# Graph attention on TensorE: exponentials as weights in column tiles of 32, V with a column of ones as 65 streaming columns

## What is computed

```
h  = max(layernorm(x), 0)                            # x is 4096 x 64
scores = (h W a1)[:, None] + (V W a2)[None, :]       # V = entity_embs, 4096 x 64
e  = where(scores > 0, scores, 0.2 scores); where(adj > 0, e, -9e15)
x  = x + elu(softmax(e, axis=1) @ V + h)
h2 = max(layernorm(x), 0)
x  = x + relu((adj.T @ h2) @ U.T / adj.sum(axis=0)[:, None])
```

## Time and profile before

| | |
|---|---|
| median of 3 runs | 402.12 us (400.76 to 402.92) |
| span of the profiled execution, first to last instruction | 399.7 us |
| the runs' times and that span | the span is 2.4 us below the median, 1.1 below the fastest run |
| PE busy | 350.8 us, 88% |
| DVE busy | 305.2 us, 76% |
| ACT busy | 258.7 us, 65% |
| POOL busy | 154.5 us, 39% |
| mean granted TensorE clock | 0.973 of 2.4 GHz |
| PE instructions | 7003 matmuls, 7003 weight loads |

### The profile page before, as it was taken

One profiled execution on the slowest core, in us unless ns is written; L12 is line 12 of the kernel. 1 busy time (PEld: TensorE's weight loads), 2 busy tenths in 40 slices (PEclk: granted clock), 3 DMA queues, 4 the chain that ended last, 5 costly groups with the idle time before them and its releaser, 6 DMA issues.

```text
span 399.7 us, 15175 instructions
## 1 busy us (share of the span) xinstructions
PE 350.8 (88%) x7003; PEld 220.2 (55%) x7003; DVE 305.2 (76%) x419; ACT 258.7 (65%) x322; POOL 154.5 (39%) x136
## 2 busy tenths in 40 slices
PE   1716999799999888889999989989997899999996
PEld 0712565454445464535455534445544448999996
DVE  8799899759998598889967989998889761307433
ACT  2402699799997888799889999967775760110000
POOL 8775385584220771130051130032569682210000
PEclk9958699999999999999999999999999999999999
DMA  9999999999999999971000010002001004201110
GB/s 168 130 108 109 108 107 114 130 107 108 109 139 104 105 107 104 103 83 50 2 4 3 4 55 3 3 8 53 3 3 29 2 4 80 55 2 32 41 23 18
DMA packets 26806, 25.18 MB, mean 63 GB/s; under 512 B 22041, under 2 KB 22105, under 8 KB 26742
## 3 DMA queue, kind: packets, MB, share of 16 engines
q0 software_dynamic: 4752, 16.90, 40.7%
q1 hardware_dynamic: 19830, 6.75, 7.7%
q10 hardware_dynamic: 2160, 0.56, 0.8%
HBM read 72.76 MB, written 2.11 MB: 187 GB/s over the span
## 4 chain that ended last, share of the span: by engine, by line
PE 44%; DVE 25%; POOL 10%; issue 9%; ACT 6%; DMA 5%; SPq 0%; POOLq 0%; DVEq 0%
DVE scratch L882 15%; PE w L1249 13%; PE q L1364 10%; PE q L1224 9%; PE den L1257 4%; PE w L1364 4%; DMA adj_sb<-in_adj_dram 3%; POOL adj_sb L425 3%; DVE arena L934 3%; ACT q L724 2%; ACT arena L710 2%; DMA bi<-rows_sb 1%; PE den L1364 1%; POOL adj_sb L429 1%; POOL stat_c L470 1%
## 5 line engine op out<-in xcount | busy, mean ns | idle before, releaser
L882 DVE CUSTOM_DVE_ANT_0 scratch<-adj_sb,t_row 125x2048 uint8<-125x2048 uint8 x66 | 152.9, 2317 | 4.6 <-DMA adj_sb<-in_adj_dram 1.7
L1249 PE MATMUL w<-arena,v_sb 128*32 128x500 f32 (+3 forms) x1120 | 128.8, 508 | 2.3 <-issue 1.3
L1224 PE MATMUL q<-bi,adj_sb 128*32 128x125 bf16 (+1 forms) x3360 | 93.1, 220 | 15.2 <-ACT q L724 7.7
L1224 PEld LDWEIGHTS q<-bi,adj_sb 128*32 128x32 fp8e4 (+1 forms) x3360 | 70.8, 97 | 63.6 <-ACT q L724 32.2
L706 ACT ACTIVATE arena<-q,t_col 128x1000 f32<-128x1000 f32 (+2 forms) x102 | 88.4, 871 | 7.9 <-PE q L1224 7.6
L1257 PE MATMUL den<-arena,ones 128*32 128x250 f32 (+1 forms) x960 | 80.5, 342 | 0.0
L1257 PEld LDWEIGHTS den<-arena,ones 128*32 128x32 f32 x960 | 38.2, 111 | 49.8 <-issue 45.2
L710 ACT ACTIVATE arena<-arena,t 128x1000 f32<-128x1000 f32 (+2 forms) x38 | 40.8, 1073 | 18.6 <-DVE arena L934 18.4
L724 ACT ACTIVATE q<-second_row,minus_b 128x750 f32<-128x750 f32 (+1 forms) x49 | 48.1, 981 | 1.3
L724 ACT ACTIVATE q<-arena,minus_b 128x375 f32<-128x375 f32 (+1 forms) x53 | 42.3, 800 | 1.3
L1364 PE MATMUL q<-g_all,adj_sb 124*128 124x129 f16 (+1 forms) x660 | 39.2, 220 | 0.0
(11 more groups left out here) (186 smaller groups left out, 376.8 us busy)
## 6 DMA issues: line engine op xcount, KB each, us to landing
adj_sb<-in_adj_dram POOLq DMA_DIRECT2D x33, 500.0 KB, 37.0
arena<-s_dram SPq DMA_DIRECT2D x2, 500.0 KB, 7.8
out_dram<-v_sb SPq DMA_DIRECT2D x10, 96.0 KB, 1.9
x_sb<-in_x_dram SPq DMA_DIRECT2D x1, 928.0 KB
v_sb<-x_dram SPq DMA_DIRECT2D x1, 768.0 KB, 5.3
v_sb<-n_L_gnn_entity_embs_dram ACTq DMA_DIRECT2D x2, 256.0 KB, 5.7
v_sb<-n_L_gnn_entity_embs_dram SPq DMA_DIRECT2D x2, 256.0 KB, 4.8
second_row<-s_dram SPq DMA_DIRECT2D x1, 500.0 KB, 4.3
```

The lines of the kernel that those rows point to most:

```text
L882: nc.vector.tensor_tensor_reduce(out=junk[0:R, :], in0=adj_bytes[0:R, b, half], in1=t_row[0:R, half], scale=1.0 / ONE, scalar=0.0, op0=ALU ...
L1224: last = nc.tensor.matmul(q[n % Q_SLOTS][e:e + width, bank, start:start + R], weights, bi[:, i % BI_SLOTS, k, :], start=not ON_ACT[n] and ...
L1249: last = nc.tensor.matmul(att(i)[h * D + d:h * D + d + 32, 0:(k1 - k0) * R], v_sb[:, c, d:d + 32], e[:, k0 * R:k1 * R], start=first, stop= ...
```

## The change

**Weighing.** The operands are swapped. The exponentials of a tile, 32 columns at a time (`E_COLUMNS`; 32, 32, 32 and 29 of a block's 125), are the weights; V's chunk with a 65th column of ones (`v_sb` grows by one column, filled once by a memset) streams through, 65 columns. The result lies in natural rows in `w`, with the row sum as column 65 of each block. `ones32`, `sel4`, `den`, `copy_att`, `copy_den`, `to_natural`, `pair` and `weigh_pair` go, and `e` has three slots in every group.

**Masks** are cut in column tiles of 32 in all groups.

**Closing** starts with `normalise`, which reads `w` as soon as the last tile is weighed, and every step of `WHEN` moves a few tiles ahead. The product with U and the small transposes get banks of `w` of their own. After the last tile the first four gathers run ahead of `turn_h2`.

```diff
-    MASK_COLUMNS = (128, 128, 32, 32, 32)
+    MASK_COLUMNS = (32, 32, 32, 32, 32)
...
+    E_COLUMNS = 32
...
-        v_sb = sb("v_sb", [P, NC, D])
+        v_sb = sb("v_sb", [P, NC, D + 1])
...
-        den = ps("den", [P, 512])
-        w = ps("w", [P, 3, 512])
+        w = ps("w", [P, 4, 512])
...
+            nb = GROUPS[i][1] - GROUPS[i][0]
+            n_banks, in_bank = (2, nb // 2) if nb > 4 else (1, nb)
+            return w[:, i % 2 * 2:i % 2 * 2 + n_banks, 0:in_bank * (D + 1)].rearrange("p h (k d) -> p h k d", d=D + 1)
...
-            for m in range(PAIRS):
-                pair(m)
...
+            close(LAST - 1)
             close(LAST)
...
             def normalise(i):
...
-                dve.wait_ge(natural, i + 1)
...
+                dve.wait_ge(weighed, NC * (i + 1))
+                nc.vector.tensor_tensor(den8[0:R, 0:nb].rearrange(by_bank, h=banks_of), att(i)[0:R, :, :, D],
+                                        empty[0:R, b0:b1].rearrange(by_bank, h=banks_of), ALU.add).then_inc(den_done, 1)
...
             def attend(n, i, c):
 
                 nb = GROUPS[i][1] - GROUPS[i][0]
+                in_bank = nb // 2 if nb > 4 else nb
                 e = e_slot(n, nb)
                 pe.wait_ge(exped, n + 1)
...
-                for h, (k0, k1) in enumerate(((0, half), (half, nb))):
-                    for d in range(0, D, 32):
-                        last = nc.tensor.matmul(att(i)[h * D + d:h * D + d + 32, 0:(k1 - k0) * R], v_sb[:, c, d:d + 32],
-                                                e[:, k0 * R:k1 * R], start=first, stop=final)
...
-                for k, (k0, count) in enumerate(quarters(nb)):
-                    last = nc.tensor.matmul(den[32 * k:32 * k + 32, 0:count * R], ones32[:, :], e[:, k0 * R:(k0 + count) * R],
-                                            start=first, stop=final)
+                for k in range(nb):
+                    bank, place_in = k // in_bank, k % in_bank
+                    for e0 in range(0, R, E_COLUMNS):
+                        e1 = min(e0 + E_COLUMNS, R)
+                        last = nc.tensor.matmul(att(i)[e0:e1, bank, place_in, :], e[:, k * R + e0:k * R + e1], v_sb[:, c, :],
+                                                start=(c == 0 and place_in == 0), stop=(c == NC - 1 and place_in == in_bank - 1))
                 last.then_inc(weighed, 1)
...
-            gather(0, 0, late)
-            to_natural(NI - 1)
-            for o in (1, 2, 3):
+            for o in (0, 1, 2, 3):
                 gather(o, 0, late)
```

More of the change, by code:

```diff
@@ L67, in graph_layers_kernel @@
     WHEN = {
[L68 to L81, removed]
+        'normalise': (None, 2, 2, 2, 2),
+        'exp_hp': (None, 9, 5, 4, 5),
+        'elu': (None, 4, 7, 5, 6),
+        'elu_below': (None, 6, 7, 6, 8),
+        'square': (None, 14, 11, 10, 11),
+        'spread': (None, 12, 12, 12, 13),
+        'scale': (None, 17, 14, 14, 16),
+        'turn_h2': (None, 19, 17, 18, 18),
+        'copy_h2': (None, 20, 17, 21, 18),
+        'times_u': (None, 22, 19, 23, 20),
+        'high': (None, 24, 21, 24, 21),
         'sum_s': (12, 1, 4, 2, None),
@@ L284, in e_slot @@
         def e_slot(n, nb):
[L286 to L292, removed]
+            return arena[:, n % E_SLOTS, 0:nb * R]
         def e_part(n, nb):
@@ L659, in copy_rows @@
                 act.wait_ge(a_made, 1)
[L660 to L669, removed]
+                nc.scalar.activation(a_part(0, nb), first_rows(), ACT.Copy).then_inc(a_copied, 1)
             def exp_hp(i):
@@ L1069, in _ @@
                         row_shifts(i + 1)
-            copy_den(NI - 1)
             normalise(NI - 1)
@@ L1160, in turn_shifts @@
                 for k in range(nb):
-                    bank, start = place(nb, k)
-                    last = nc.tensor.matmul(pair_of(0)[96:P, bank, start:start + R], turn[0:R, k, :], ident16[0:R, 0:R],
+                    last = nc.tensor.matmul(first_rows()[96:P, k * R:(k + 1) * R], turn[0:R, k, :], ident16[0:R, 0:R],
                                             start=True, stop=True)
@@ L1173, in turn_halves @@
                     pe.wait_ge(u_copied, 3)
-                nc.tensor.matmul(z1[32:32 + 2 * nb, 2 * P:2 * P + R], halves[0:R, 0:2 * nb], ident16[0:R, 0:R], start=True, stop=True)\
+                nc.tensor.matmul(across(i)[32:32 + 2 * nb], halves[0:R, 0:2 * nb], ident16[0:R, 0:R], start=True, stop=True)\
                     .then_inc(halves_turned, 1)
@@ L1194, in rows @@
                 for k in range(b1 - b0):
-                    bank, start = place(b1 - b0, k)
-                    last = nc.tensor.matmul(pair_of(0)[:, bank, start:start + R], s08[0:R, b0 + k:b0 + k + 1].to_broadcast([R, P]),
+                    last = nc.tensor.matmul(first_rows()[:, k * R:(k + 1) * R], s08[0:R, b0 + k:b0 + k + 1].to_broadcast([R, P]),
                                             ident[0:R, 0:R], start=True, stop=True)
@@ L1352, in _ @@
                 attend(n, *TILES[n])
-            for m in range(PAIRS - 3, PAIRS):
-                weigh_pair(m)
             def gather(o, first, last_one):
```

173 lines of the change are left out of this document (39 added, 134 removed).

## The result

The changed kernel takes **532.21 us** (median of 4 runs, 525.87 to 534.55) where the kernel before, measured alongside, takes 402.52 us (median of 4 runs, 400.76 to 403.32). The ratio is **1.316, with a 95% interval of 1.308 to 1.325**: slower by a third. The ratio leaves out the run of 534.55 us, which was in the slower of the chip's two states, so it is a little under the quotient of the two medians. The forecast was 505 us with a range of 430 to 560.

What follows compares the result with a forecast made beforehand. PE was taken to be bound by code loads, one per 256 instructions: groups end at 432, plus 4 to the first gather, 63 gathers and 3.5 end, 502.5; the median 2.4 above gives 505 us, range 430 to 560.

Steps and rivals of the forecast that it cites:

- Streaming: PE's work on a tile of 8 blocks: weighing 0.93 us, with masks 1.40 instead of 1.73 us.
- Group 0: 2320 instructions, 9.1 blocks at 6.0 us after the first: end at about 92 us, 12 later than before.
- Loaded T: Time from requesting a 256-instruction code block until it can run, while adjacency loads fill the DMA engines: 6.0 us.
- Group 1 and the late loads: 18.5 code blocks, end 183 us; the last four adjacency loads slow 3.3 blocks, +9: 192 where 135.8 was.
- Groups 2 to 4: 6200 instructions each, 24.2 code blocks at 3.3 us: 80 us each, 240 in place of 189.5.
- free T: Time from requesting a code block until it can run, without adjacency loads: 1.1 + 0.95 + 1.3, taken as 3.3 us.
- The upper bound of 3.95: Limit on the code-block time without adjacency loads: a block's worth ran in 3.94 us in group 4 without a stop.
- the tail: From the last mask to the end: 4 us to the first gather, gathers 63, end 3.5.
- Rival 1: Whole kernel: code is no bound and streaming arithmetic rules, so it gets faster, 380 us; chance 6%.
- rival 2: Code binds only while adjacency loads run; groups 2 to 4 take 62 + 61 + 48, 435 us; chance 15%.
- Rival 3: Weighing: fp32 weight loads of four column tiles don't run side by side, round 114 ns, 430 us; chance 3%.
- The clock: PE's clock dropping in the pauses: no rival; a block at half clock about 3.4 us, some 10 us over the sum.

Runs made afterwards that it cites:

- x3: The changed kernel streaming 33 of V's 65 columns in all but the first tile of a group, same instruction count: 534.74 us, ratio 1.329.
- x4: The kernel before with V's weighing cut in pieces of 125 columns, same data streamed by more instructions: 426.9 us, ratio 1.061.
- x6: The kernel before with the masks of groups 0 and 1 in column tiles of 32 instead of 128: 409.31 us, ratio 1.018.
- x1: The changed kernel with column tiles of 64 instead of 32 for both weighing and masks: 388.66 us, ratio 0.966.
- x2: The changed kernel with column tiles of 64 in the weighing alone, masks still 32: 420.64 us, ratio 1.046.

## Why the prediction was right, and where its size was off

**What bounds the kernel.** Right. PE runs dry at the end of each block of 256 instructions and is one block ahead at most: 109 code loads as forecast, stretches of exactly 128 + 128, the load of the next block 1.1 us after a block is entered. x3 shows that streaming time does not set the pace here, x4 and x6 that instructions alone slow the old kernel, x1 that the same data with half the instructions is faster than before. The rule of the Trainium skill ("Runtime: NRT & Kernel Launch", Instruction fetch mechanics) that a crossing is mostly hidden does not hold for this kernel: 163.4 us of stops stand against it.

**Streaming.** Right: 0.91 us for a weighing where 0.93 was forecast, 1.37 us of work in a tile for 1.40.

**Group 0** came to 53.4 us for 54.7. Loaded T was 5.9 to 6.5 with a median of 6.2 for the 6.0 taken.

**Group 1 and the late loads.** The sum for group 1 was 91 without the late adjacency loads and 9 for them; it took 93.5. The last four loads came, but later: they ran from about 183 to 204 us, in group 2, as the stretches at 189 and 195 show (DMA share 0.98 to 1.03, blocks of 6.4 and 7.0 us); the block before these, from 182.1, took 7.0 us as well. That was a matter of place: tile 28 of 32 comes near the end of a group of 93 us, and the loads follow it. The prediction's "about 64" instructions of a tile of group 1 before was also wrong: 6 masks and 8 fp32 matmuls are 2 x 6 + 4 x 8 = 44. No term of the sum used it.

**Groups 2 to 4: the term that was mis-sized is free T.** The prediction took 3.3 us from 1.1 + 0.95 + 1.3. The three parts measured 1.2, 1.1 and 1.4 on average, so each was 0.1 to 0.15 short. The middle one came from one load of 0.95 us, which was a short one: loads of the free stage take 0.9 to 1.5 us. T is 3.73. With 24.2 blocks a group that is 24.2 x 0.43 = 10 us for each, 31 in all. Measured against forecast: group 3 +7.1, group 4 +9.4, group 2 +17.9, of which some 8 are the late loads that moved here. The upper bound of 3.95 from the earlier trace rows held for the median, though single blocks took up to 4.02, and the range reached there.

**The sum.** Starts and groups come to 458.1 for 432, +26.1; the tail 72.9 for 70.5, +2.4, of which one stop in the gathers is 1.5; the median stands 1.2 above the span for the 2.4 taken, -1.2. Together +27.3, from 505 to 532.2.

**The rivals.** Rival 1 (code no bound, 380) and rival 2 (code binds only beside adjacency loads, 435) fall with the stops that go on through groups 3 and 4 at a DMA share of 0.05. Rival 1's arithmetic was near, though: x1, in which code seldom binds, came to 388.7 for its 380 and has groups 3 and 4 near what it named (63.3 and 48.7; it had forecast 61 and 48), while group 2, where x1 still stops at block ends, took 68.9 for 62. Rival 3 (fp32 loads one after another, a round of 114 ns) falls with a round of 57 ns, in x1 with twice the columns too.

**The clock.** It fell more than the earlier trace rows would suggest: the granted clock was 0.70 and 0.66 on average in groups 0 and 1, and 0.50 (1.2 GHz) between 189 and 202 us, after a stretch of 7.0 us in which PE worked for 2.0. The prediction took 3.4 us for a block at half clock and gave this some 10 us; from its own 1.40 us a tile it should have been 1.40 x 256 / 192 x 2 = 3.7. A block's work is 3.6 to 3.7 us there, still under the 6.4 and 7.0 that the block takes, so the lower clock is hidden in the wait for code.

## What to carry to other kernels

Count PE's instructions, not only its columns: an fp32 matmul is four of them here, and a block of 256 took at least 3.4 us (3.7 in the median) where code set the pace, and 5.9 (6.2) while loads filled the DMA engines. A row of stops with releaser "issue", 256 instructions apart, is the sign, even if there are only six of them and PE looks 88% busy. When operands are cut into column tiles, take the widest tile whose weight load still hides in a round: 64 columns did all that 32 did, with half of the instructions. 128 columns were not tried for the exponentials.

## What the runs showed of the hardware that was not expected

- The load of one 16 KB code block takes between 0.9 and 1.5 us with the DMA engines free; one window is not enough to size it.
- While adjacency loads fill the DMA engines, the load of code itself takes 0.9 to 1.0 us and no longer; it begins late, 3.5 to 4.3 us after the block is entered instead of 1.0 to 1.7 (groups 0 and 1 against groups 2 to 4 of the changed kernel).
- The fp32 weight load of 64 columns hides under 65 streaming fp32 columns as well as that of 32 does (0.91 us for a weighing in both).
- Changing between column tiles of 32 and of 64 twice a tile cost 0.28 us (x2); whether each change costs a fixed time was not tried.
- Cutting a matmul of 500 columns into four of 125 costs PE 0.02 us in 0.84 where no block ends (x4).
